# Second cross attention: the maximum subtracted in PSUM by a matmul, exp from PSUM, and the mix as alternating 64-row matmuls into four banks

## Reference

```
q = (text_hidden @ Wq).reshape(B, T_text, 16, 128)       # 16 heads
k = (vision_tokens @ Wk).reshape(B, T_vis, 8, 128)       # 8 heads, each for two of q
v = (vision_tokens @ Wv).reshape(B, T_vis, 8, 128)
scores = jnp.einsum('bhtd,bhsd->bhts', q, k) / sqrt(128)
scores = jnp.where(mask, scores, -jnp.inf)
attn = softmax(scores, axis=-1)
out = jnp.einsum('bhts,bhsd->bhtd', attn, v)
out = out.reshape(B, T_text, 16 * 128) @ Wo
x = x + tanh(g_xattn) * out                               # the gate of the second layer
```

## Time and profile before

| | |
|---|---|
| time, median of 3 runs | 533.88 us (533.27 to 535.6) |
| profiled execution, first to last instruction | 530.4 us |
| time beside its span | 3.5 us (533.88 less 530.4) |
| PE matmul busy | 443.2 us (84%) |
| VectorE busy | 362.0 us (68%) |
| ScalarE busy | 199.5 us (38%) |
| GpSimd busy | 170.8 us (32%) |
| mean granted TensorE clock | 0.889 |

### The profile page before, as it was taken

How to read it: one execution, slowest core, us unless ns; L and a number is a source line. 1 busy time by engine, 2 the same in 40 slices (tenths; PEclk the granted TensorE clock), 3 DMA queues, 4 the chain that set the end, 5 groups by cost and what they waited for, 6 DMA issues and landing times.

```text
span 530.4 us, 8960 instructions
## 1 busy us (share of the span) xinstructions
PE 443.2 (84%) x2992; PEld 399.9 (75%) x2992; DVE 362.0 (68%) x785; ACT 199.5 (38%) x390; POOL 170.8 (32%) x204
## 2 busy tenths in 40 slices
PE   0575948666468999999998999989999998989996
PEld 0455837555468889898997978968998896888886
DVE  5768688695506557585757698698788779855542
ACT  2355535363221333233233534454344344423331
POOL 3004132232300221212123453564454365333322
PEclk9958886959556999999899969998996998999999
DMA  8111010100200020010201001001000100000000
GB/s 242 30 59 59 1 59 0 60 2 6 93 1 0 1 99 0 15 83 0 99 0 53 1 0 53 1 0 51 0 0 1 50 0 0 0 0 21 20 20 21
DMA packets 6628, 15.96 MB, mean 30 GB/s; under 512 B 1090, under 2 KB 4291, under 8 KB 6100
## 3 DMA queue, kind: packets, MB, share of 16 engines
q1 hardware_dynamic: 6612, 15.75, 9.1%
HBM read 14.70 MB, written 1.05 MB: 30 GB/s over the span
## 4 chain that ended last, share of the span: by engine, by line
PE 51%; issue 17%; DVE 13%; POOL 11%; ACT 4%; DMA 3%; POOLq 0%; DVEq 0%; ACTq 0%; SPq 0%
PE ps L287 34%; DVE work L1277 4%; PE ps L1071 3%; PE ps L468 3%; POOL work L1329 2%; POOL workr L1453 2%; PE ps L803 2%; POOL workA L554 2%; PE ps L458 2%; PE ps L824 2%; PE ps L827 1%; POOL wB_lo L560 1%; PE ps L258 1%; DMA stage<-in_wC 1%; PE ps L1083 1%
## 5 line engine op out<-in xcount | busy, mean ns | idle before, releaser
L287 PE MATMUL ps<-xT_hi,wB_hi 128*128 128x256 f32 x224 | 67.7, 302 | 1.7 <-POOL wB_lo L1334 1.7
L287 PE MATMUL ps<-xT_lo,wB_hi 128*128 128x256 f32 x224 | 64.6, 289 | 0.0
L287 PE MATMUL ps<-xT_hi,wB_lo 128*128 128x256 f32 x224 | 64.4, 288 | 0.0
L287 PE MATMUL ps<-wB_hi,workr 128*128 128x256 f32 (+1 forms) x224 | 52.4, 297 | 3.8 <-POOL workr L1453 3.4
L287 PE MATMUL ps<-wN_hi,shared_r 128*128 128x256 f32 x256 | 52.7, 301 | 0.0
L995 POOL TENSOR_TENSOR workr<-work,workr 128x256 fp32r<-128x256 f32 (+1 forms) x36 | 22.9, 636 | 83.8 <-ACT workr L878 83.8
L287 PEld LDWEIGHTS ps<-xT_hi,wB_hi 128*128 128x128 f32 x224 | 44.1, 197 | 4.0 <-issue 1.9
L1329 POOL TENSOR_SCALAR work<-work,lut_step,lut 128x344 f32<-128x344 int32 (+1 forms) x72 | 46.5, 660 | 1.6 <-POOL wB_lo L1334 1.6
L1277 DVE COPY_PREDICATED work<-work 128x1376 f32<-128x1376 int32 (+5 forms) x36 | 43.6, 1212 | 4.0 <-DVE work L1277 1.1
L287 PEld LDWEIGHTS ps<-wN_hi,shared_r 128*128 128x128 f32 x256 | 43.9, 206 | 1.5 <-DVE shared_r L1240 1.5
L287 PEld LDWEIGHTS ps<-xT_lo,wB_hi 128*128 128x128 f32 x224 | 44.2, 197 | 0.0
(11 more groups left out here) (178 smaller groups left out, 1161.3 us busy)
## 6 DMA issues: line engine op xcount, KB each, us to landing
stage<-in_wC SPq DMA_DIRECT2D x4, 1280.0 KB, 5.4
stage<-in_wB SPq DMA_DIRECT2D x4, 768.0 KB, 4.3
stage<-in_idx SPq DMA_DIRECT2D x4, 536.0 KB, 4.0
stage<-in_wA SPq DMA_DIRECT2D x2, 512.0 KB, 5.6
out<-x SPq DMA_DIRECT2D x4, 256.0 KB, 2.2
x<-in_x SPq DMA_DIRECT2D x1, 768.0 KB, 7.2
ctx_T<-in_ctx_T SPq DMA_DIRECT2D x1, 512.0 KB, 7.6
ctx_n<-in_ctx_n SPq DMA_DIRECT2D x4, 128.0 KB, 2.2
```

The costliest lines, as they stand in the source:

```text
L287: last = nc.tensor.matmul(out, l, r, start=start and i == 0, stop=stop and i == 2)
```

## The change

The subtraction on VectorE goes. VectorE writes the negated maximum (`neg_max`), and a new TensorE step `shift` adds it to the scores where they lie in PSUM: the identity times the negated maximum, each repeated 64 times. ScalarE's exp then reads PSUM and writes `pC`. So the scores' banks come free after the exp. The mask value becomes 2^100, and mask and ones are 128 rows deep (127 of the mask's are zero). The mix is cut in two (one per tile), its matmuls alternate between the sequence in rows 0 to 63 and that in rows 64 to 127, and z has four banks. The turned probabilities of the second half use the banks the other way round. The order changes on all but GpSimd, and `output(0, 1)` is cut in two.

```diff
-MASKED = 1e30
+MASKED = 2.0 ** 100
...
-        mask_rows = sb("mask_rows", [1, 2, TG], BF16)
-        ones_row = sb("ones_row", [1, P], BF16)
+        mask_rows = sb("mask_rows", [P, 2, TG], BF16)
+        ones_row = sb("ones_row", [P, P], BF16)
...
+            nc.vector.memset(mask_rows, 0.0).then_inc(mask_cleared, 1)
...
-        TURNED = (5, 0)
+        TURNED = ((5, 0), (0, 5))
...
-            return ps[:, (6, 7, 1)[n % 3], :]
+            return ps[:, (6, 7, 1, 5)[n % 4], :]
...
+            def scores(u, s):
...
+                if u:
+                    pe.wait_ge(*C["exp_ready"].at(g, s + 1))
...
+            def shift(u, s):
+
+                n = 2 * u + s
+                pe.wait_ge(*C["maxed"].at(g, n + 1))
+                nc.tensor.matmul(ps[:, 3 + s, :].rearrange("p (k n) -> p k n", k=8), ident_r, bc_last(neg_max[:, n, :], S),
+                                 start=False, stop=True, skip_group_check=True).then_inc(*C["shifted"].up())
...
-                if n >= 2:
-                    pe.wait_ge(*C["pT_lo"].at(g, n - 1))
+                if n == 2:
+                    pe.wait_ge(*C["pT_lo"].at(g, 2))
+                if n == 3:
+                    pe.wait_ge(*C["z_lo"].at(g, BG))
...
-                        if n >= 3:
-                            pe.wait_ge(*C["z_lo"].at(g, n - 2))
-                        r = slice(S * b, S * b + S)
-                        mm3(z_of(n), cx_hi[r, t, :], cx_lo[r, t, :], pT_hi[r, t, :], pT_lo[r, t, :],
-                            True, True).then_inc(*C["z_done"].up())
...
+                if u:
+                    pe.wait_ge(*C["z_lo"].at(g, n - 2))
+                top, low = slice(0, S), slice(S, 2 * S)
+                nc.tensor.matmul(z_of(n), cx_hi[top, t, :], pT_hi[top, t, :], start=True, stop=False)
+                nc.tensor.matmul(z_of(n + 1), cx_hi[low, t, :], pT_hi[low, t, :], start=True, stop=False)
+                nc.tensor.matmul(z_of(n), cx_hi[top, t, :], pT_lo[top, t, :], start=False, stop=False)
+                nc.tensor.matmul(z_of(n + 1), cx_hi[low, t, :], pT_lo[low, t, :], start=False, stop=False)
...
-            queries(0)
-            scores(0)
-            queries(1)
+            every, first, second = range(HALF), range(HALF // 2), range(HALF // 2, HALF)
+            for j in range(PAIRS1):
+                queries(j)
+            scores(0, 0)
+            scores(0, 1)
+            queries(PAIRS1)
+            shift(0, 0)
+            queries(PAIRS1 + 1)
+            shift(0, 1)
+            queries(PAIRS1 + 2)
+            queries(PAIRS1 + 3)
             turn_probs(0, 0)
             turn_probs(0, 1)
-            scores(1)
-            mix(0)
+            scores(1, 0)
+            scores(1, 1)
+            mix(0, 0)
+            shift(1, 0)
+            mix(0, 1)
+            shift(1, 1)
+            output(0, 0, every)
             turn_probs(1, 0)
-            output(0, 0)
             turn_probs(1, 1)
-            output(0, 1)
+            output(0, 1, first)
+            mix(1, 0)
+            output(0, 1, second)
+            mix(1, 1)
             front_pe(pe, 9 + g, 3)
-            mix(1)
-            output(1, 0)
-            output(1, 1)
+            output(1, 0, every)
+            output(1, 1, every)
...
-                v = split_tokens(pC[:, s])
-                nc.scalar.activation(v, v, ACT.Exp, scale=HD1 ** -0.5).then_inc(*C["exp_ready"].up())
+                if u:
+                    act.wait_ge(*C["pT_done"].at(g, s + 1))
+                nc.scalar.activation(split_tokens(pC[:, s]), ps[:, 3 + s, :], ACT.Exp,
+                                     scale=HD1 ** -0.5).then_inc(*C["exp_ready"].up())
...
-                nc.vector.tensor_reduce(mxC[:, n, :], sc, AX, ALU.max).then_inc(*C["maxed"].up())
-                dve.wait_ge(*C["maxed"].at(g, n + 1))
-                if u:
-                    dve.wait_ge(*C["pT_done"].at(g, s + 1))
-                nc.vector.tensor_tensor(pC[:, s], sc, bc_last(mxC[:, n, :], S),
-                                        ALU.subtract).then_inc(*C["shifted"].up())
+                nc.vector.tensor_reduce(neg_max[:, n, :], sc, AX, ALU.max, negate=True).then_inc(*C["maxed"].up())
```

More of the change, by code:

```diff
@@ L1008, in build @@
         pC = take(2 * 512).rearrange("p (s k n) -> p s k n", s=2, k=8)
-        mxC, smC, rcC = (take(4 * 8).rearrange("p (s n) -> p s n", s=4) for _ in range(3))
+        smC, rcC = (take(4 * 8).rearrange("p (s n) -> p s n", s=4) for _ in range(2))
         bits = take(4 * RMAX).bitcast(I32).rearrange("p (b n) -> p b n", b=4)
@@ L1058, in scores, with queries @@
-            def scores(u):
-                if u == 0:
-                    pe.wait_ge(*C["mask_ready"].at(g, 2))
-                for s in range(2):
-                    if u:
[L1064 to L1074, removed]
+            def queries(n):
+                if n >= 2:
+                    pe.wait_ge(*C["q_ready"].at(g, n - 1))
+                for h in range(2):
+                    hh = 2 * n + h
+                    for c in range(DC):
+                        last = mm3(q_of(n)[:, h * TG:(h + 1) * TG], wM_hi[:, hh, c * DV:(c + 1) * DV],
+                                   wM_lo[:, hh, c * DV:(c + 1) * DV], xT_hi[:, c, :], xT_lo[:, c, :],
+                                   c == 0, c == DC - 1)
+                last.then_inc(*C["q_done"].up())
@@ L1107, in output @@
+            def output(u, t, heads):
+                if heads[0] == 0:
+                    pe.wait_ge(*C["z_lo"].at(g, u * BG + 2 * t + 2))
+                    if t == 0:
+                        pe.wait_ge(*C["x_done"].at(g, u))
+                for h in heads:
                     hh = u * HALF + h
@@ L1183, in act_C @@
             level1(1)
+            upper_z(0, 0)
             exps(1, 0)
-            upper_z(0, 0)
             upper_z(0, 1)
@@ L1197, in act_C @@
             upper_z(1, 3)
+            front_upper(act, 9 + g, 3)
             upper_decoded(2)
@@ L1210, in dve_C, with top @@
                                         ALU.mult).then_inc(*C["ctx_masked"].up())
-            def shift(u, s):
+            def top(u, s):
                 n = 2 * u + s
@@ L1280, in dve_C @@
             front_norm(dve, 9 + g, after(g))
-            shift(0, 0)
-            shift(0, 1)
+            top(0, 0)
+            top(0, 1)
             sums(0, 0)
@@ L1290, in dve_C @@
             lower_probs(0)
-            shift(1, 0)
-            shift(1, 1)
+            top(1, 0)
+            top(1, 1)
             lower_z(0, 0)
+            lower_z(0, 1)
             sums(1, 0)
-            lower_z(0, 1)
             sums(1, 1)
```

65 lines of the change are left out of this document (33 added, 32 removed).

## The result

| | before | after |
|---|---|---|
| time, median (runs) | 533.58 us (4; 531.72 to 535.6) | 545.26 us (4; 544.4 to 545.63) |
| profiled span | 530.4 us | 543.2 us |
| mean granted TensorE clock | 0.889 | 0.896 |

The changed kernel takes 1.0226 of the time of before, with an interval of 1.0199 to 1.0254. It is slower, by 2.0 to 2.5%, and 544.1 was forecast. The medians differ by 11.7 us and the spans by 12.8, since the profiled execution of before was faster than its median.

A forecast was written before the change was run, and what follows sets the result against it. A loop sets the pace: scores, VectorE's chain to `lower_probs(1)`, `mix(1)`, outputs, next queries. New order 6.7, clock 3.2 and identity copy 0.3 gave 10.2 us on 533.88, so 544.1; range 539.3 to 549.3.

The forecast's parts named there:

- The first shift: First half of each group: shift matmul of 0.25 us stands behind a query, making VectorE 1.85 us late at `choose(0)`.
- Middle: From `choose(0)` to `choose(1)`: two saved subtractions (1.4 us) almost make up the delay, yet `choose(1)` starts 1.5 us late.
- Before `mix(1)`: Moving `lower_probs(1)` ahead of `take_bits(2)` gains nothing; TensorE waits 3.5 us and `mix(1, 0)` starts 0.3 us later.
- Tail: End of a group: half of `output(0, 1)` and the turn stand behind `mix(1, 0)`, so outputs end 2.1 us late.
- The clock: TensorE's wait invites a clock fall at `mix(1)`: 0.8 us per group, 3.2 in all, range 0 to 6.8.
- the term of the chain: Lateness of the new order over the groups: 2.1 us in two, 1.25 in the other two, 6.7 in all.
- The sum: Whole span: 6.7 us from the new order, 3.2 from clock falls, 0.3 for an identity copy; 10.2 us slower.
- The signs: New profile: first exp about 2.5 us later behind the scores, VectorE busy 11 us less, groups lasting 46 to 47.5.
- The mixes and the rest: Mix matmuls already overlap; four banks remove the wait for `z_lo`; deep mask 0.1 us each if anything; identity copy 0.3.
- VectorE's saving comes through: VectorE paces the group and the shift slips in unseen: 11.1 us go, 522.8 us, decided at `choose(0)`; chance 0.08.
- Slack swallows it: Late `choose(1)` still meets the same `mix(1)`, the clock stays up, groups keep 43.9 to 44.9 us: 534; chance 0.08.

The follow-up runs named there:

- d_early_shift: The changed kernel with the two first-half shifts moved forward, the first directly behind the second scores, the other between halves of the first query; 537.75 us.
- e_old_tail: The changed kernel with the end of each group in the old order on all three engines, whole `output(0, 1)` ahead of `mix(1, 0)`; 534.54 us.
- a_grouped_mix: The changed kernel with each batch of six mix matmuls in the old order, three and three, instead of alternating; 547.14 us.
- g_before_banks: The kernel before with four z banks, turned probabilities swapped in the second half and the alternating mix, keeping subtraction and order; 532.23 us.
- c_before_deep_mask: The kernel before with mask and ones 128 rows deep instead of one, nothing else changed; 533.04 us.
- i_order_sub: The changed kernel's parts reordered, but with the subtraction on VectorE and exp in place as before, in an order found for that; 520.72 us.
- f_both: The changed kernel with both repairs together, the early shifts and the old tail order; 532.51 us.
- h_order_mm: All parts of the changed kernel, shift by matmul included, with the order of TensorE, ScalarE and VectorE written anew; 523.61 us.

## Why the prediction was right, step by step

- **The first shift.** The slot measured 0.21 us (346.16 to 346.37), 0.25 was taken. exp out of PSUM takes 600 ns, 0.633 was taken. The place was the cost, as put: waits of 1.6 and 0.7 us on VectorE before its sums (1.8 and 0.8 forecast), 1.16 us on TensorE before `queries(6)` (1.35 forecast). d_early_shift, which only moves the shifts, wins 7.5 us. `choose(0)` is 1.44 us late; 1.85 was forecast, and the deep mask, costed at next to nothing, took 0.5 off.
- **Middle.** `choose(1)` starts 28.67 us into the group against 27.52: 1.15 late, 1.5 forecast, for the same reason.
- **Before `mix(1)`.** A wait of 3.3 us (3.5 forecast), and `mix(1)` at 34.79 us of the group against 34.86; 0.3 late was forecast. The moved `lower_probs(1)` gained nothing, as said: it waits 1.12 us for ScalarE.
- **Tail.** `output(1, 0)` starts 40.69 us into the group against 38.18: 2.5 late, 2.1 forecast. Against before all of the loss shows here: `mix(1)` starts at most 0.3 us later than in before in any group, but from the start of `mix(1)` to `output(1, 0)` the four groups of after take 6.50, 5.90, 7.26 and 7.25 us, and those of before 3.3 each. The path leads through the first batch of the mix, the half of `output(0, 1)`, two `lower_z` and the add. In the second group the clock costs 0.74 of it, since the half output takes 2.19 us where it was costed at 1.45; the second batch is slow too (1.57 instead of 0.90), but nothing on this path waits for it. Without the clock the path takes 5.16 us in this group, and 5.15 to 5.17 in the others; 5.1 were forecast (367.2 to 372.3). e_old_tail wins 10.7 us and shows that the tail is where most of the loss arises.
- **The clock.** This term of the sum was mis-sized: 0.8 us a group, 3.2 in all. On the path above, the matmuls at the lower level cost 1.35, 0.74, 2.09 and 2.08 us in the four groups, 6.3 in all. I had made 3.41 us the most that a fall behind the wait lasts; in two groups it lasted 6.8. The rest of the 12.67 us, 6.4, is the term of the chain, forecast at 6.7, with the 1.3 us in it that the first group lost to the clock at its beginning.
- **The sum.** 12.8 us on the span stand against 10.2 forecast. That the time misses by only 1.2 is in part luck. I took 3.5 us for what the time has beyond the span by setting a median against an execution faster than it; in the four runs of after it is 1.8 to 2.1. The medians rose by 11.7.
- **The signs.** The first exp starts 2.3 us later behind the end of the first scores than before (3.82 against 1.55; 2.5 forecast), VectorE's busy time falls by 10.3 us (11), and the groups last 46.4 to 48.3 us (46 to 47.5), the longest being those with the clock's larger losses.
- **The mixes and the rest.** Right: a_grouped_mix and after show the overlap in both orders, and g_before_banks has 1.4 us for the banks and all that came with them. The deep mask was under-priced as a slot (0.25 saved, 0.1 taken), though c_before_deep_mask shows that in before it brings nothing.

The rival in which VectorE's saving comes through fell at its own test, `choose(0)`. It falls a second time with i_order_sub: between the orders found there the saving is worth nothing. "Slack swallows it" was right about `mix(1)` and wrong about what stands behind it.

The losses are not additive. The late shift and the late tail give 7.5 and 10.7 us when undone alone and 12.7 together. The last column of the table fits that: undoing both leaves 23.4 us at the lower clock, as many as after has, while d has 20.0 and e 13.2. Taken at half, the clock's part is 1.7 us in d's gain and 5.1 in e's, which leaves 5.8 and 5.6 us of waiting; together 11.4, near the 12.7. That is an estimate; no run holds the clock.

## What to carry to other kernels

When an operation moves from a busy engine to a loaded one, cost what stands ahead of it there and what stands behind its consumer first, and the operation itself last: here the moved work was 0.2 us and its place 1.4. In a kernel whose engines run written orders, find the order for the new work before judging the work; the same work took 190 and 163 us in this stage. Look then at what the next stage waits for, since 3.3 of these 27 us came back there. And before expecting a saved wait in the time, look at how long TensorE stays at the lower clock level afterwards.

## What the runs showed of the hardware

- Eight fp32 matmuls behind a one-row mask matmul take 0.1 to 0.2 us more than behind a 128-row one, and the first of them starts 0.1 later.
- fp32r matmuls of 64 rows on different row halves start in pairs, within 0.04 us of each other, whether they are issued alternating or three and three, and take the same 0.90 us for six.
- COPY_PREDICATED of 1376 columns took 1.77 us in one place of h_order_mm and 2.67 in another. That the second lies beside GpSimd's work was read from the trace and not tested.
- Shorter waits of TensorE did not mean less time at the lower clock: f_both has 6.83 us in each of three groups, before and after have 3.41 to 10.2 in a group, and h_order_mm has none in groups two to four.
